# Expert outputs: scatters that add to cleared rows in place of scatters that write over them

## What is computed

```python
weights, selected = jax.lax.top_k(gate_logits, TOP_K)          # TOP_K = 2, 4096 tokens
weights = jax.nn.softmax(weights)
flat_experts = selected.reshape(-1)
sort_idx = jnp.argsort(flat_experts)
sorted_x = jnp.take(x, sort_idx // TOP_K, axis=0)
h0 = jax.lax.ragged_dot(sorted_x, w0, group_sizes)             # 64 experts, 256 -> 512
h1 = jax.lax.ragged_dot(sorted_x, w1, group_sizes)
out_sorted = jax.lax.ragged_dot(jax.nn.silu(h0) * h1, wo, group_sizes)
unsorted = jnp.take(out_sorted, jnp.argsort(sort_idx), axis=0)
out = jnp.einsum('BKE,BK->BE', unsorted.reshape(4096, TOP_K, 256), weights)
```

## Time and profile before

| | us |
|---|---|
| median of 3 runs (lowest, highest) | 1332.15 (1330.96, 1334.1) |
| the profiled execution | 1334.92 |
| its span, from first to last instruction | 1333.2 |

### The profile page before, as it was taken

The page is one execution under the profiler, slowest core; times in us unless marked ns, Lnnn a source line. Parts: engine busy times, 40 slices in busy tenths (PEclk is TensorE's granted clock), DMA queues, the critical chain, the costliest instruction groups (busy, mean ns, idle before and its releaser), DMA issues. The chain is left out here.

```text
span 1333.2 us, 21073 instructions
## 1 busy us (share of the span) xinstructions
PE 1051.0 (79%) x6867; PEld 931.6 (70%) x6867; DVE 922.2 (69%) x2071; ACT 577.5 (43%) x1286; POOL 637.2 (48%) x609
## 2 busy tenths in 40 slices
PE   5767878787887875777826886999999999989970
PEld 4656767677776765666412775899999888888860
DVE  6999999999999993888786897233332333222348
ACT  3768787877778672443601652212212111111110
POOL 4886978888786960200003552344344443433420
PEclk8899899999999898555767996899999999999985
DMA  8544546464646532022130112888788788877729
GB/s 241 188 141 140 172 139 198 137 192 151 188 160 187 168 105 66 17 48 32 32 125 2 56 49 76 289 270 274 260 269 279 259 270 274 266 262 262 253 94 352
DMA packets 161165, 231.41 MB, mean 174 GB/s; under 512 B 32157, under 2 KB 85773, under 8 KB 160417
## 3 DMA queue, kind: packets, MB, share of 16 engines
q1 hardware_dynamic: 145520, 206.67, 49.2%
q0 software_dynamic: 9200, 18.96, 4.1%
q10 hardware_dynamic: 6336, 4.44, 1.0%
HBM read 203.01 MB, written 22.80 MB: 169 GB/s over the span
## 5 line engine op out<-in xcount | busy, mean ns | idle before, releaser
L1010 PE MATMUL st_y_ps<-ident,st_hc 128*128 128x128 f32 x2048 | 274.8, 292 | 110.8 <-DVE st_hc L529 110.8
L1010 PEld LDWEIGHTS st_y_ps<-ident,st_hc 128*128 128x128 f32 x2048 | 256.8, 204 | 132.9 <-DVE st_hc L529 132.1
L412 POOL TENSOR_TENSOR st_u<-st_dx,codes 128x1024 f32<-128x1024 f32 x127 | 296.4, 2359 | 39.3 <-DVE st_h L521 31.5
L521 DVE TENSOR_TENSOR_SCAN st_h<-st_da,st_u 128x512 f32<-128x512 f32 x256 | 297.6, 1203 | 0.2 <-POOL st_u L412 0.2
L2279 PE MATMUL mo_h<-mo_xt,w 128*128 128x128 f32 (+17 forms) x2048 | 284.2, 290 | 2.0 <-DVE mo_xt L2402 2.0
L2279 PEld LDWEIGHTS mo_h<-mo_xt,w 128*128 128x128 f32 x2048 | 273.7, 194 | 6.7 <-issue 2.7
L2408 DVE TENSOR_TENSOR mo_inter<-mo_silu,mo_h 128x128 f32<-128x128 f32 (+17 forms) x256 | 75.5, 303 | 280.2 <-ACT mo_silu L2361 217.6
L2361 ACT ACTIVATE mo_silu<-mo_h 128x128 f32<-128x128 f32 (+17 forms) x256 | 71.6, 290 | 315.5 <-PE mo_h L2279 224.9
L2220 POOL DMA_INDIRECT outs<-mo_o,choice x95 | 93.7, 986 | 234.8 <-DVE mo_o L2419 221.0
L748 ACT ACTIVATE st_da<-st_delta,st_a_neg 128x510 f32<-128x510 f32 x256 | 172.1, 685 | 58.3 <-DVE st_h L521 53.7
L529 DVE TENSOR_TENSOR st_hc<-st_h,st_cps 128x1024 f32<-128x1024 f32 x128 | 152.5, 1192 | 0.0
(11 more groups left out here) (393 smaller groups left out, 1437.5 us busy)
## 6 DMA issues: line engine op xcount, KB each, us to landing
codes<-bc SPq DMA_DIRECT2D x256, 256.0 KB, 3.7
w<-in_L_ffn_w_dram SPq DMA_DIRECT2D x128, 512.0 KB
wo<-in_L_ffn_wo_dram SPq DMA_DIRECT2D x64, 512.0 KB
co_got<-outs SPq DMA_DIRECT2D x16, 512.0 KB, 6.1
wave<-dist SPq DMA_DIRECT2D x16, 274.0 KB
x<-in_x_dram SPq DMA_DIRECT2D x8, 512.0 KB, 9.1
st_cx<-in_ctx_dram SPq DMA_DIRECT2D x8, 512.0 KB, 4.0
dist<-st_dd SPq DMA_DIRECT2D x32, 128.0 KB, 3.4
```

The lines of the kernel that those rows point to most:

```text
L412: nc.gpsimd.tensor_tensor(u_sb[k % URING][:, :, :], dx[p % 2][:, :, :], over_chunks(b_sb[k % BRING]), ALU.mult).then_inc(u_ok, 1)
L521: nc.vector.tensor_tensor_scan(h_sb[k % HRING][:, dh, :], da_ps[dh][:, :], u_sb[k % URING][:, dh, :], 0.0, ALU.mult, ALU.add).then_inc(h_o ...
L1010: m = nc.tensor.matmul(y_ps[t // 2][:, t % 2, dh * P:(dh + 1) * P], hc_sb[k % RING][:, dh, t * P:(t + 1) * P], K.ident[:, :], start=False, ...
```

## The change

VectorE first fills a tile `zero` of 128 x 256 with zeros. SyncE stores it over the 8192 rows of `outs` in 16 stores of 512 KB (128 partitions, four rows of 1 KB each, all four from the same 1 KB of SBUF), one ahead of its wait for each batch of `xn`, and waits near the end of the stage until all have landed. Each of the 95 scatters of the unrolled turns then carries an add: the DMA reads the row of `outs`, adds the expert's row, and writes the sum. The scatter of the late loop (line 2241 before) is as it was: it writes over its rows. Two waits on `reach_ok` are raised by one, because the fill now counts there first.

```diff
+        zero = sb("ex_zero", [P, D])
+        cleared = sem("ex_cleared")
 ...
         def _(sp):
+            sp.wait_ge(reach_ok, 1)
             for b in range(B):
+                sp.dma_start(K.outs_dram[b * 2 * L:(b + 1) * 2 * L, :].rearrange("(p r) d -> p r d", p=P),
+                             zero[:, :].rearrange("p (r d) -> p r d", r=1).broadcast_to([P, 4, D])
+                             ).then_inc(cleared, 16)
                 sp.wait_ge(xn_ok, b + 1)
                 sp.dma_start(K.xn_dram[b * L:(b + 1) * L, :].rearrange("(t p) d -> p t d", p=P),
                              xn[b % 4][:, :, :]).then_inc(xn_out[b % 4], 16)
             sp.wait_ge(row_ok, ORDER)
             load_weights(K, sp, expert_at(K, sp, 0), 0)
+            sp.wait_ge(cleared, 16 * B)
 ...
-            pool.wait_ge(reach_ok, 2)
+            pool.wait_ge(reach_ok, 3)
 ...
+            nc.vector.memset(zero[:, :], 0.0).then_inc(reach_ok, 1)
             did(nc.vector.tensor_tensor(mid[:, :, :], K.hi[:, :, :], K.lo[:, :, :], ALU.add))
 ...
-            act.wait_ge(reach_ok, 1)
+            act.wait_ge(reach_ok, 2)
 ...
                     nc.gpsimd.indirect_dma_start(K.outs_dram[:, :],
                                                  bass.IndirectOffsetOnAxis(ap=K.choice[0:n, at:at + 1], axis=0),
-                                                 o_sb[k % XR][0:n, a, :], None).then_inc(o_out[k % XR], 16)
+                                                 o_sb[k % XR][0:n, a, :], None,
+                                                 compute_op=ALU.add).then_inc(o_out[k % XR], 16)
```

## The result

| | before | changed |
|---|---|---|
| measured together, median | 1333.12 us (1330.96 to 1335.77, 4 runs) | 1307.62 us (1307.14 to 1308.07, 4 runs) |
| span of the profiled execution | 1333.2 us | 1305.8 us |
| ratio | | 0.9815, 95% interval 0.98 to 0.9829 (the two medians alone: 0.981) |

The forecast was no measurable difference, 1332.4 us.

The account below looks back on a forecast made before the run. The prediction took TensorE to bound `experts`, with transfers beside it. Fill 0.2, clears 0 and adding scatters 0 us on the 1332.15 us median gave 1332.4 us, no measurable difference; range 1330.5 to 1338 us.

Parts of the forecast that it names:

- What bounds the kernel: In `experts` TensorE, busy 287.27 of 300 us, sets the pace; scatters, gathers and loads run beside it.
- Hidden, so 0 on the path at either bound: GpSimd's longer issue of adding scatters in `experts` costs no time, whether 0 or 1.0 us more each.
- the fourth: Rival, faster: only a shift in how VectorE and GpSimd get in each other's way; some 1329 us, chance 0.03.
- The fill: Zero tile filled first on VectorE in `expand`, delaying `mid` and the path by 0.2 us, bounds 0.1 and 0.42.
- The clears: The 16 clearing stores in `expand` fit beside the `xn` stores: 0 us, bounds 0 and 4.
- GpSimd's issue: In `experts` an adding scatter takes about 0.1 us more to issue, bounds 0 and 1.0; hidden.
- The DMA engines: In `experts` an add costs 0.047 us more a row, some 6 points of DMA share; 0 on the path.
- The first rival: Slower: few adding packets under way make DMA engines the bound in `experts`; 1353 us at five, chance 0.13.
- the third rival: The add costs just what a plain scatter does, leaving only the zero tile's fill: 1332.4 us, chance 0.1.
- The landing: Adding scatters land before buffers are reused and 12.3 us before they would be last ahead of the read-back: 0 us.
- The sum: Over the whole kernel 0.2 + 0 + 0 = +0.2 us, bounds 0.1 and 4.4; forecast 1332.4 us.

Follow-up runs that it names:

- plain_filler: The kernel before with a GpSimd memset of about 0.65 us behind every scatter, plain scatters and no clears: 1307.0 us, ratio 0.971.
- half_pauses: The kernel before with a GpSimd memset of about 0.35 us behind each indirect issue, gathers and scatters alike: 1307.4 us, ratio 0.9709.
- short_weights: The kernel before with SyncE's weight transfers cut to an eighth of each matrix from the fifth expert on: 1348.0 us, ratio 1.0009.
- plain_early_scatter: The kernel before with the narrow expert's plain scatter issued ahead of the gather that stood before it: 1326.5 us, ratio 0.9855.
- adds_early_scatter: The changed kernel with the narrow expert's adding scatter issued ahead of the gather that stood before it: 1307.1 us, ratio 0.9688.

## Why the prediction was wrong

**What bounds the kernel: the step that failed.** "So TensorE sets the pace of `experts`, and scatters, gathers and loads run beside it." TensorE did set the pace, but its 18.3 us of waits were taken as its own pipeline's, and the waits behind them were not followed. One step back stood ScalarE, which started its third activation 2.59 us after the matmuls for it, and beside it in the timeline GpSimd's issues at 1.3 us. GpSimd was priced by whether it is late itself (2.3 us more for each scatter), and never by what its issuing does to other engines. So "Hidden, so 0 on the path at either bound" was wrong in sign: 0.6 us more for each scatter spread the issues and gave 28.3 us back. Of these, TensorE's waits account for 18.3 - 1.0 = 17.3 us. The rest counts as busy, because ends of matmuls are modelled, but lies at the same places: from the start of one matmul to that of the next, the steps into the second and the third down-projection took 8.4 and 14.4 us more in the wide turns before than after, and the first steps within these two 3.7 us more, 26.5 of the 28.3 us.

**The rival that came true** was the fourth, a shift in how engines get in each other's way, with 0.03 and some 1329 us. It named VectorE and GpSimd. So it came true in its general form and not by its engines. What is late in the traces is what TensorE releases: VectorE's `mo_inter` still followed ScalarE's activation at once (1111.90 + 0.29, then 1112.23). No term was worked out for it, and its size was a guess.

**The fill** held: 0.27 us, and `mid` 0.21 us later, against the 0.2 taken. VectorE at the start of `expand`:

```profile
720.52 0.27 DVE L1756 MEMSET ex_zero<- 128x256 f32 x1 [0.64 <-PEq L1313]
720.83 0.19 DVE L1757 TENSOR_TENSOR ex_mid<-hi,lo 128x32 f32<-128x32 f32 x1
```

**The clears** were taken at 0, with 0 and 4 us as bounds. A clear lands in 3.2 us, the DMA share of the beats is 0.42 as forecast. From `mid` to the first up-projection matmul the profiled executions of the two kernels differ, 116.27 us before and 117.81 after, but not because of the clears: over the 13 traces of kernels without clears this stretch takes 115.8 to 118.2 us, 117.1 in the mean, and over the 7 with them 116.1 to 117.9, 117.0 in the mean. No cost of the clears shows, and the 0 held.

**GpSimd's issue** of an adding scatter was mis-sized: +0.1 us taken, 1562 - 977 ns = +0.59 measured, within the bounds of 0 and 1.0. The changed kernel's issues from 900 to 1250:

```profile
L2228 POOL DMA_INDIRECT outs<-mo_o,choice x83 | 129.7, 1562 | 119.1 <-DVE mo_o L2428 102.3 <-issue 16.8
L2221 POOL DMA_INDIRECT mo_xg<-xn,table x78 | 77.3, 991 | 23.8 <-issue 23.8
```

The estimate went from the price of 120 more rows, 0.12 us in the earlier trace rows, to that of a third address for each row. The add made the issue 0.59 us longer, whatever GpSimd does in it.

**The DMA engines.** Queues of the changed kernel from 900 to 1200 (packets, MB, share of 16 engines), as in the earlier trace rows:

```profile
q1 hardware_dynamic: 49582, 72.62, 72.4%
q0 software_dynamic: 12114, 13.52, 22.0%
```

Queue 0 takes 22.0% of 16 x 300 us = 1056 us for 13,200 rows. At the 0.047 us of a copied row that would be 620; about half of the rows are scatters, so an add costs some 436 / 6600 = 0.066 us more for a row. I took 0.047, with 0.21 as the point where DMA becomes the bound. The share of 1100 to 1200 is 0.97, against 0.88 in plain_filler and 0.90 in half_pauses at the same pace: about 0.08, and 0.06 was forecast. The forecast of 0.85 to 0.87 was missed because the stage itself became faster.

**The first rival**, few adding packets under way, did not come: no wait of TensorE for a DMA. Queue 0 has twice the packets: in the records of single packets an added row has one of its own, 1 KB in some 102 ns, where a plain scatter's carries four rows in 159 ns. That is 62 ns more a row, as worked out above, and nowhere near 0.25 us. The Trainium skill's sentence in "DMA: Bandwidth & Descriptors", section "Two DMAs through the same engine are not ordered", on two read-modify-write packets to one row with five or more packets between them, is not contradicted by this, and no run here tests it. What I made of it, about five under way at 0.30 us a row, is contradicted: the row took 0.047 + 0.066 = 0.11 us. The same rows decide against the third rival, by which an add costs just what a plain scatter does. That an add reads its row is not to be seen in the profile's count of HBM reads, which is 203.01 MB in both kernels.

**The landing** held. The late scatter at the end of the chain (start us, us):

```profile
1265.71 2.48 DMA outs<-mo_o,mo_to
...
1268.26 3.97 DMA co_got<-outs
```

2.48 us and then the read-back, where the earlier trace rows has 2.44.

**The sum.** Forecast +0.2. Measured by parts on the two profiled executions: -28.3 in the wide turns, -0.4 in the narrow ones, +1.75 up to the first up-projection matmul (836.89 to 838.64; 0.21 of it is the fill, the rest within the spread given under the clears), together -27.0; the spans differ by 27.4.

## What to carry to other kernels

When the bounding engine's waits end on another engine, follow them one engine further: an engine that starts late although its releaser has been done for 2 us has not been waiting for that work, and something else in the same microseconds has to be found. GpSimd's indirect transfers were not free here, though GpSimd had time to spare: look at how far apart their issues stand, and try a filler of 0.4 us behind each, which here gave 2.9% (half_pauses, beside a kernel before of 1345.8 us). And before a gain is put down to what a change is for, copy only its timetable: a kernel with plain scatters and pauses reached the same time.

## What the runs showed of the hardware

- While GpSimd issued three or more indirect transfers of 128 rows one after the other, every 1.3 to 1.5 us, releases from TensorE came late in wide turns: to ScalarE by up to 3.6 us in the kernel before and 3.8 us in short_weights, to VectorE by up to 1.6 us in plain_early_scatter. With issues 1.67 us apart (half_pauses) no activation was late, nor in adds_early_scatter, where the third of three gathers in a row, at 5.4 us, comes behind the fourth activation. The changed kernel, with an adding scatter of 1.6 us between two gathers, has up to 0.6 us at the third activation. One wide turn of the kernel before (the one that starts at 1095.10) has its scatter at 2.31 us instead of 0.97, for no reason that the trace shows; it has no late activation and takes 6.18 us, where the next wide turn takes 7.51.
- It needs indirect issues and no traffic: lag 171.0 us with DMA engines at 0.22, and 6.3 us with the same gathers as direct transfers, whose issue takes GpSimd 0.58 us.
- Narrow turns of the kernel before are spared. There the four activations start at 1.1, 2.0, 3.3 and 4.6 us, and GpSimd issues at 3.5, 4.8 and 6.1 us: three activations come ahead of its first issue, and the fourth when only one issue has gone out.
- How an issue on GpSimd holds up a release from TensorE is open: no view of the trace shows what lies between. TensorE may not be the only one held up. The third load that SyncE issues in a wide turn, with no wait ahead of it, comes at 2.7 to 2.8 us in most wide turns of the kernel before, and at 1.9 us in the one that starts at 1095.10 and in most of half_pauses.
- The issue of an adding scatter of up to 128 rows took GpSimd 1.56 us in the mean, a plain one 0.98.
